# A routed FFN on one core: b1 written into PSUM by ScalarE, weights read in place at register offsets

## What is computed

```python
def cond(x, y, weight, mask, bias):                 # x (2,1024,256), y (2,8)
    w_bot = einsum('bg,got->bot', y, weight * mask)
    return einsum('bnt,bot->bno', x, w_bot) + bias

def ffn(x, gate_w, gate_b, w1, b1, w2, b2):         # 2048 tokens, 8 experts, D=256, H=1024
    logits = xf @ gate_w.T + gate_b
    top1 = argmax(logits, axis=-1)
    for e in range(8):
        h = relu(xf @ w1[e].T + b1[e])
        y = h @ w2[e].T + b2[e]
        out = out + where(top1 == e, y, 0)

result = x + ffn(cond(x, ...), ...)
```

## Time and profile before

| | us |
|---|---|
| median of 3 runs | 203.94 |
| fastest, slowest of the 3 | 201.84, 204.02 |
| span of the profiled execution | 202.2 |

### The profile page before, as it was taken

One profiled execution on the slowest core, in us unless ns is written; L12 is line 12 of the kernel. 1 busy time (PEld: TensorE's weight loads), 2 busy tenths in 40 slices (PEclk: granted clock), 3 DMA queues, 4 the chain that ended last, 5 costly groups with the idle time before them and its releaser, 6 DMA issues.

```text
span 202.2 us, 6441 instructions
## 1 busy us (share of the span) xinstructions
PE 170.4 (84%) x1810; PEld 135.6 (67%) x1811; DVE 131.3 (65%) x229; ACT 103.0 (51%) x158; POOL 123.4 (61%) x119
## 2 busy tenths in 40 slices
PE   0076988838879999999999999999999999999810
PEld 0026657723468888888888888888888878887700
DVE  0499498996799888896996768886542424542200
ACT  2400865750188855687898787642356222325000
POOL 7294699704814882935557488888776775456310
PEclk9996589985999999999999999999999999999995
DMA  4999911730696677677666731122122111111100
GB/s 105 375 411 409 402 50 59 238 129 26 157 387 239 231 244 241 231 232 233 212 217 220 254 105 52 32 68 79 35 78 82 65 50 50 32 40 45 40 22 0
DMA packets 12242, 31.24 MB, mean 154 GB/s; under 512 B 3055, under 2 KB 5295, under 8 KB 12088
## 3 DMA queue, kind: packets, MB, share of 16 engines
q1 hardware_dynamic: 8552, 24.46, 34.9%
q0 software_dynamic: 3024, 6.30, 10.1%
q10 hardware_dynamic: 640, 0.17, 0.4%
HBM read 27.99 MB, written 4.88 MB: 163 GB/s over the span
## 4 chain that ended last, share of the span: by engine, by line
PE 74%; DVE 15%; DMA 3%; issue 2%; DVEq 1%; SPq 1%; POOL 0%; ACT 0%; ACTq 0%; POOLq 0%
PE psum L957 29%; PE psum L974 28%; PE psum L951 6%; PE psum L891 4%; DVE stage L626 4%; DMA wsp<-cond_w 3%; PE psum L941 2%; PE psum L847 2%; PE psum L925 1%; DVE offs L704 1%; DVE padded L700 1%; DVE wsp L645 1%; PE psum L876 1%; DVE wsp L668 1%; DVE stage L650 1%
## 5 line engine op out<-in xcount | busy, mean ns | idle before, releaser
L957 PE MATMUL psum<-xs,stage 128*128 128x128 f16 x1008 | 63.6, 219 | 0.0
L957 PEld LDWEIGHTS psum<-xs,stage 128*128 128x128 f16 x1008 | 56.4, 98 | 9.5 <-issue 9.5
L974 PE MATMUL psum<-stage,hT 128*128 128x256 f16 x336 | 56.2, 273 | 1.4 <-DVE res L790 0.8
L974 PE MATMUL psum<-wsp,hT 128*128 x168 | 45.8, 273 | 0.0
L458 POOL DMA_INDIRECT res<-x_rows,tok_of_slot x21 | 25.8, 1228 | 30.0 <-DMA out<-res,tok_of_slot 26.1
L452 POOL DMA_INDIRECT xg<-xf_rows,tok_of_slot x21 | 28.4, 1351 | 20.9 <-issue 12.3
L784 DVE SCALAR_TENSOR_TENSOR hT<-psum,hT 128x512 f16<-128x512 f32 x42 | 27.4, 685 | 18.6 <-ACT hT L588 14.6
L974 PEld LDWEIGHTS psum<-stage,hT 128*128 128x128 f16 x336 | 31.7, 98 | 5.7 <-issue 2.2
L674 DVE SCALAR_TENSOR_TENSOR wsp<-wsp x25 | 30.5, 1257 | 5.0 <-issue 4.5
L588 ACT ACTIVATE hT<-psum 128x512 f16<-128x512 f32 x42 | 23.6, 592 | 17.2 <-PE psum L957 13.8
L579 ACT ACTIVATE xs<-psum,bias_col 128x128 f16<-128x128 f32 x42 | 13.1, 364 | 33.2 <-PE psum L941 29.6
(11 more groups left out here) (118 smaller groups left out, 157.7 us busy)
## 6 DMA issues: line engine op xcount, KB each, us to landing
wsp<-w_all SPq DMA_DIRECT2D x32, 512.0 KB
wsp<-cond_w SPq DMA_DIRECT2D x4, 512.0 KB, 7.1
wsp<-x_t SPq DMA_DIRECT2D x2, 1024.0 KB, 10.8
b_all<-b SPq DMA_DIRECT2D x1, 1024.0 KB, 8.2
xf_rows<-stage SPq DMA_DIRECT2D x1, 768.0 KB, 3.8
xf_rows<-stage SPq DMA_DIRECT2D x1, 640.0 KB, 3.3
xf_rows<-stage SPq DMA_DIRECT2D x1, 384.0 KB, 3.1
xg<-xf_rows,tok_of_slot POOLq DMA_INDIRECT x21
```

The lines of the kernel that those rows point to most:

```text
L957: last = t_.matmul(o, w1s[:, b, w:w + P], xs[:, b, xp, k * P:(k + 1) * P], start=False, stop=(c % 4 == 3 and k == KD - 1 and wp == 1))
L974: last = t_.matmul(ps_y[b], hT[:, b, hp, c * P:(c + 1) * P], w, start=(c == 0 and w is high and hp == 0), stop=(c == KH - 1 and w is low))
```

## The change

ScalarE writes 64 times b1 into both PSUM banks of a tile (`seed_h`), one tile ahead, from `b1_col`, which the host lays out with one column per slice of H; the matmuls of layer 1 then add to it (`start=False`). PE first writes each of the four banks once (`primed`), in place of four of the 26 filling matmuls. The bias matmul, `b1_parts`, `chunk_of`, the split of b1 and its way through HBM are gone. `w1s`, `w2s` and both copies are gone too: each matmul of both layers reads W1 and W2 in `wsp`, at an offset in a register. PE now waits itself for the splits of W1 (`lo_late`), and reads `tile_plan`.

```diff
@@ GpSimd: memset b1_parts, chunk_of and its two affine_selects removed; SyncE: b1_scratch, b1_parts DMAs removed
@@ ScalarE
-            act.dma_start(b1_raw[:, :], b1).then_inc(ld_b1, 16)
+            act.dma_start(b1_col[:, :], b1).then_inc(ld_b1, 16)
-            act.wait_ge(ld_b1, 16)
-            a.mul(b1_split[:, 0, :], b1_raw[:, :], WSCALE).then_inc(b1_high, 1)
-            def w2_copy(i, b, plan):
...
+            def seed_h(i, b, e):
+
+                if late(i, 2):
+                    act.wait_ge(hlo_ready, 2 * i - 2)
+                a.mul(psum[:, 1 + 2 * b:3 + 2 * b, :].rearrange("p q (c n) -> p (q c) n", n=P),
+                      b1_col[:, bass.ds(e * KH, KH)].unsqueeze(2).to_broadcast([P, KH, P]), WSCALE).then_inc(h_seeded, 1)
+
+            act.wait_ge(ld_b1, 16)
+            act.wait_ge(primed, 1)
+            seed_h(0, 0, plan.next_expert)
+            x_hi(0, 0)
             split_chunks(act, high_late, 0, plan.goal)
-            x_hi(0, 0)
-                if_used(act, used, i, lambda: w2_copy(i, b, plan))
+                if_used(act, used, i + 1, lambda: seed_h(i + 1, 1 - b, plan.next_expert))
@@ VectorE
-            def w1_copy(i, b, plan):
...
-            for n in range(FIRST_STORES):
-                dve.wait_ge(rows_stored[n], 16)
-            with dve.If(plan.next_expert == 0):
-                w1_into(0, 0)
...
-                if_used(dve, used, i + 1, lambda: w1_copy(i + 1, 1 - b, plan))
@@ TensorE
-            keep_clock_up(26)
+            keep_clock_up(22)
+            for q in range(4):
+                last = t_.matmul(psum[:, 1 + q, :], ones_h[:, :], ones_h[:, :].unsqueeze(1).to_broadcast([P, 4, P]),
+                                 start=True, stop=True)
+            last.then_inc(primed, 1)
-            pe.wait_ge(b1_ready, 32)
-            def layer1(i, b, e):
-                pe.wait_ge(w1_ready, i + 1)
+            def layer1(i, b, plan):
+                e = plan.next_expert
+                pe.wait_ge(lo_late, plan.goal + AHEAD)
                 pe.wait_ge(xlo_ready, i + 1)
-                if late(i, 2):
-                    pe.wait_ge(hlo_ready, 2 * i - 2)
+                pe.wait_ge(h_seeded, i + 1)
                 for c in range(KH):
-                    if c % 4 == 0:
-                        t_.matmul(ps_h[b][c // 4], b1_parts[:, bass.ds(e, 1), c // 4, :].rearrange("p o m -> p (o m)"),
-                                  chunk_of[:, :, :], start=True, stop=False)
                     o = ps_h[b][c // 4][:, (c % 4) * P:(c % 4 + 1) * P]
                     for k in range(KD):
                         for wp, xp in ((0, 0), (0, 1), (1, 0)):
-                            w = k * 2 * CH + wp * CH + c * P
-                            last = t_.matmul(o, w1s[:, b, w:w + P], xs[:, b, xp, k * P:(k + 1) * P],
-                                             start=False, stop=(c % 4 == 3 and k == KD - 1 and wp == 1))
+                            w = wsp[:, bass.ds(e * (CPE * 2 * CH) + k * 2 * CH + wp * CH + c * P, P)]
+                            last = t_.matmul(o, w, xs[:, b, xp, k * P:(k + 1) * P],
+                                             start=False, stop=(c % 4 == 3 and k == KD - 1 and wp == 1),
+                                             skip_group_check=True)
@@ layer2
-                pe.wait_ge(w2_ready, i + 1)
...
+                    high = wsp[:, bass.ds(e * (CPE * 2 * CH) + chunk * 2 * CH + c * D % CH, D)]
                     low = wsp[:, bass.ds(e * (CPE * 2 * CH) + chunk * 2 * CH + CH + c * D % CH, D)]
-                    high = w2s[:, b, c * D:(c + 1) * D]
@@
+            pe.wait_ge(lo_pool, POOL_SPLITS)
             turn_x(0, 0, 0, 1)
...
-                e = pe.value_load(tile_expert[0:1, bass.ds(i, 1)], min_val=0, max_val=E - 1)
...
+                plan = Plan(pe, i - 1)
```

More of the change, by code:

```diff
@@ L77, in build @@
     xf_rows = nc.dram_tensor("xf_rows", [TOK, D], F32, kind="Internal").ap()
-    b1_scratch = nc.dram_tensor("b1_scratch", [2, E * KH, P], F16, kind="Internal").ap()
     with ExitStack() as ctx:
@@ L146, in build @@
         gate_bias = sb("gate_bias", [P, 1])
[L149 to L152, removed]
+        b1_col = sb("b1_col", [P, E * KH])
         ident = sb("ident", [P, P])
@@ L222, in build @@
         x16_lo_ready = [sem(f"x16_lo_ready{n}") for n in range(4)]
-        b1_ready = sem("b1_ready")
+        primed = sem("primed")
+        h_seeded = sem("h_seeded")
         gate_ps = sem("gate_ps")
@@ L260, in build @@
         y_ready = sem("y_ready")
-        N_CONST = 12
+        N_CONST = 11
         RANKS_AFTER = 3
@@ L363, in _ @@
                 confirm(q, LOADED // CPE)
[L364 to L368, removed]
             sp.wait_ge(x_in[1], 16)
@@ L374, in _ @@
             sp.wait_ge(rows_ps, TT)
-            sp.wait_ge(b1_ready, 32)
             for n in range(len(STORES)):
@@ L398, in _ @@
             g.memset(ones[:, :], 1.0).then_inc(consts, 1)
[L399 to L406, removed]
             acc = wbot[:, 1, :, :].rearrange("p k n -> p (k n)")
@@ L470, in scatter @@
                                      bounds_check=TOK - 1, oob_is_err=False).then_inc(stored[i % RING], 16)
-            pool.wait_ge(pool_step, 7)
+            pool.wait_ge(pool_step, 4)
             for n in range(len(STORES)):
@@ L553, in _ @@
             act.wait_ge(experts_known, 1)
-            def w2_copy(i, b, plan):
-                act.wait_ge(hi_ready, plan.goal + EARLY)
-                if late(i, 2):
[L558 to L572, removed]
             def x_hi(i, b):
@@ L755, in _ @@
             dve.wait_ge(tok_ps, 1)
-            def w1_into(b, expert):
-                v.tensor_copy(w1s[:, b, :], wsp[:, bass.ds(expert * (CPE * 2 * CH), CPL * 2 * CH)]).then_inc(w1_ready, 1)
-            def w1_copy(i, b, plan):
-                dve.wait_ge(lo_late, plan.goal + AHEAD)
-                if late(i, 2):
-                    dve.wait_ge(h_ps, 2 * i - 2)
-                    with dve.If(plan.next_same == 0):
-                        w1_into(b, plan.next_expert)
-                    with dve.Else():
-                        dve.wait_ge(w1_ready, i)
-                        dve.nop().then_inc(w1_ready, 1)
-                else:
-                    w1_into(b, plan.next_expert)
             def x_lo(i, b):
@@ L806, in _ @@
                 low(n)
-            for n in range(FIRST_STORES, len(STORES)):
-                dve.wait_ge(rows_stored[n], 16)
             split_chunks(dve, low_late, 0, plan.goal)
-            with dve.If(plan.next_expert > 0):
-                w1_copy(0, 0, plan)
-            with dve.Else():
-                dve.nop()
             split_chunks(dve, low_late, plan.goal, plan.next_goal)
             def tile(i, b, r, turn, plan):
-                if_used(dve, used, i + 1, lambda: w1_copy(i + 1, 1 - b, plan))
                 if_used(dve, used, i + 1, lambda: x_lo(i + 1, 1 - b))
@@ L1021 @@
         "w_all": c(np.concatenate([w1_l, w2_l], axis=2)),
-        "b1": c(b1.reshape(E * KH, P)),
+        "b1": c(b1.reshape(E * KH, P).T),
         "b2": c(b2),
```

20 lines of the change are left out of this document (1 added, 19 removed).

## The result

The changed kernel takes 260.6 us (median; 259.3 to 261.2 over 4 runs), the kernel before on the same chip 204.0 us: a ratio of 1.282, 95% interval 1.274 to 1.291. It is 28% slower. The forecast was 255 us. The profiled execution's span is 257.5 us, against 202.2.

What follows compares the result with a forecast made beforehand. PE's array bound the kernel at 6.37 us a tile; afterwards its sequencer would, at 8.45. Layer 1 of tile 0 ends at 64.8, twenty tiles reach 233.8, last layer 2 237.2, branches 243.5, end 9.45: span 253, forecast 255 us, range 233 to 278.

Steps and rivals of the forecast that it cites:

- The array and its 17.6 us: PE's array: without bias matmuls it needs 5.53 us a tile, not 6.37; 17.6 us over 21 tiles if nothing takes over.
- A register instruction at 0.125 us: PE's sequencer: each register instruction among the matmuls costs 0.125 us including its gap, not the recorded 46 ns.
- The tile, 8.45 us: PE's sequencer: its stretches add up to 8.45 us a tile after the change, in place of 6.37.
- The start: Ahead of the tiles: layer 1 of tile 0 starts at about 59.8 us, against 56.31 before.
- The term for the clock: Layer 1 of tile 0: 1 us added because PE idles beforehand and then runs at the lower clock.
- The sum: Whole execution: start, tiles, last layer 2, branches and end give a span of 253 us, 255 us as median.
- The branches of the tail: PE's last tiles: 36 branches, 8.3 us in all, of which 5 us were counted.
- falling clock: Rival, 14%: PE's clock falls between the tiles, to 1.2 GHz for a third to all of the time; 272 to 304.
- Cheaper register instructions (0.104): Rival on PE's sequencer, 8%: 0.104 us per register instruction, tile 7.4 us, total 233.
- The hidden case: Rival, 6%: PE's register instructions hide under the array, POOL's late b2 addition binds next; span 197.8, 199.5 us.
- slack of some 2 us per tile: PE's sequencer before the change: 3.3 us a tile outside layer 1, then it stands before a full queue.
- The sign turns: PE's sequencer: gain becomes loss where a register instruction's price c reaches 0.082 us and the new tile equals 6.37 us.

Runs made afterwards that it cites:

- constant addresses: Changed kernel with both layers reading expert 0's weights in place at constant addresses, without the 48 register instructions a tile: 198.4 us, ratio 0.970.
- both versions with the bias write: Kernel before with ScalarE writing b1 and both copies kept: 199.3 us, ratio 0.983; changed kernel with W1's copy back: 200.1 us.
- the two with the own ring: ScalarE writes b1, VectorE's output gets a buffer ring separate from the residual's: with only W1 copied 189.9 us (0.934), with both copies 189.6 us (0.925).
- The kernel with only W2 in place: Kernel before with layer 2 reading W2 in wsp and ScalarE's copy of it gone, bias matmuls kept: 215.9 us, ratio 1.056.
- the version with the own ring: Changed kernel with W1's copy back and VectorE's output in a ring separate from the residual's, loop starting at tile 6: 189.9 us, ratio 0.934.

## Why the prediction was right

**The array and its 17.6 us.** Right: 5.52 us a tile wherever the sequencer and POOL let it (constant addresses, both versions with the bias write, the two with the own ring).

**A register instruction at 0.125 us.** Right, and the step that decided. The 672 of layer 1 stand 0.130 us apart on average over each tile's 32, most of them 0.124; about every eighth distance is some 0.03 longer. Half of them taken away gave back 0.12 us each. The record of 46 ns, by which they would hide, was no price. The Trainium skill, Perfetto Trace Analysis, section Per-engine timelines (Sequencer-only Instruction), says that such a record holds the execution alone. The trace of the changed kernel agrees, with 46 ns recorded against 124 ns from start to start. That there was a gap of 80 ns and that it belonged to the register instruction, not to the matmuls between, rested on eight rows each of the earlier trace rows; what stood among the eight of the earlier trace rows was a register operation and not, as it wrote, a wait. In the changed kernel layer 2 with 1.5 matmuls to each, and layer 1 also with 1.5, show the same 124 ns as the old layer 2 with three.

**The tile, 8.45 us.** 8.64 in a steady one. By stretches, from the sequencer's rows above and, where a tenth is too coarse, the same records' starts (117.69, 121.78, 122.62, 124.73, 126.33):

| stretch of the sequencer | predicted | measured |
|---|---|---|
| layer 1 | 4.0 | 4.1 |
| ahead of layer 2 | 0.8 | 0.8 |
| layer 2 | 2.0 | 2.1 |
| ahead of layer 1 | 1.65 | 1.6 |
| sum | 8.45 | 8.64 |

The missing 0.2 us are the longer distances and a register operation in the middle of layer 2. The prediction's terms for the pause ahead of layer 1 (1.3 less 0.12, plus four at 0.1) give 1.58 and not the 1.65 that it wrote; this slip made up for part of it. In the first tiles the pause ahead of layer 1 is 0.1 to 0.2 us longer, and layer 1 itself some 0.1 (tiles of 8.8 to 9.0).

**The start.** Layer 1 of tile 0 began at 58.38, not 59.8. ScalarE wrote b1 at 53.56, where I had put it at 54.3, and the write took 1.02 us and not 1.2; VectorE's last two splits end at 58.04. The term for the clock was right: 4.3 us without a matmul, then a granted clock of 0.50 (1.2 GHz), and layer 1 of tile 0 took 5.05 us, 0.9 more than in the tile above. Together layer 1 of tile 0 ended at 63.4, predicted 64.8.

**The sum.** From 63.4 to the end of layer 2 of the last but one tile (240.19 + 2.81 = 243.0) are 179.6 us; the prediction had 169.0 + 1.3 + 5 = 175.3. The last layer 2 ended at 247.6, 4.6 later (3.4 predicted), and the end came 9.9 us behind it (9.45). So the deviation of 4.5 us in the span is -1.4 + 4.3 + 1.2 + 0.4; that it had put the start 1.4 us too late hid part of what it had too little for the tiles, and that was luck. The branches of the tail, put at 5 us, were 5: the tail's tiles take 9.1 to 9.6 us, 3.8 above five steady ones, and the last layer 2 another 1.2. What was too small is the tile: 0.2 us in each, and a bit more in the first ones and behind the loop's branches (three tiles of 8.9 to 9.4).

**The rivals.** The clock stayed at 1.00 through the tiles, with the array idle for some 1.5 us in each 8.6 us: no falling clock. Cheaper register instructions (0.104) did not come. The hidden case did not come either. The kernel with constant addresses, where the 48 are gone, ended at 196.7 us against its 197.8, by the kind of wait that it named. That it is so close is partly luck: the array's last layer 2 ended at 182.0 and not at 184.8, since the array lost 3 us in three tiles and not the whole gain up to 121.4, and POOL's last scatter then started 6.4 us behind that end (188.45) where the rival had 4.8.

**A step that was wrong in its words.** "It has slack of some 2 us per tile. The change spends exactly this." What the sequencer has left in a tile of 6.37 us cannot be spent as one sum. The kernel with only W2 in place had 1.0 us more sequencer work, well within the 2 us, and lost 11 us. In the prediction's sum this did no harm, because there the sequencer was the longer in every stretch but layer 2. But the rule for the sign is doubtful: "The sign turns where 48 x c + 2.45 = 6.37, at c = 0.082" compares whole tiles. The prediction took the queue to hide some 30 matmuls. The sequencer's lead of 1.0 to 1.15 us is some 18 to 20 matmuls of 56 ns with their weight loads. The Trainium skill, TensorE: Matmul & The Clock Gate, section Architectural detail (under "Engine queue depths"), gives PE a queue of 64; no run here shows that size.

## What to carry to other kernels

Price an instruction on a sequencer by the distance between starts where the sequencer is late, never by its record, and count the addresses that stand in registers: a copy to a constant place once per tile on an engine with slack can buy off dozens of them. Compare sequencer and array stretch by stretch, each with no more than the lead of about 1 us that the sequencer had here; slack from one stretch is not there in the next. And when a bound is removed, follow what comes next before moving an order: here a buffer of its own took the wait away, where another order only exchanged it.

## What the runs showed of the hardware

- A register instruction on PE's sequencer (FUSED_REGOPS): 46 ns recorded and 124 ns from start to start, whether 1.5 or 3 matmuls lie between two. The mean in the changed kernel is 130 ns in layer 1 and 134 in layer 2, where an ALU_OP stands among them. The ALU_OP is recorded with 32 to 36 ns and is followed after some 95 ns.
- A register load from SBUF on it takes 0.30 us (0.73 once, in the kernel with only W2 in place), and with the register operation of 0.15 us behind it 0.65 us pass before the next useful instruction.
- PE's sequencer ran 1.0 us (by starts; 1.15 by the modelled ends) ahead of the array and no more, in front of matmuls of 56 ns.
- ScalarE's write of 128x1024 float32 into two PSUM banks, from a source repeated along the free axis, took 1.02 us.
- The same indirect gather occupied POOL for 1.0 or for 1.7 us in neighbouring tiles of the version with the own ring. What decides that was not tried.
